# The recurrent block of a five-stage attention network on one Trainium2 core: narrow products in pairs, packed weights, three mixture buffers, another order of units

## The chip, the core and the metric

The kernel runs on one core of one Trainium2 chip. The metric is the device time of one execution in microseconds. Each verdict rests on several runs on the same chip.

## The reference

The network works on x of 8 batches x 256 tokens x 512 features in fp32: cross attention, a channel attention, self attention, cross attention and MLP over tokens, and at last a recurrent block (RWKV-like), which is all that the change touches. Cut to what matters, for one batch (l = 256, e = 512, 32 heads of 16):

```python
xa = ln(x); sx = shift(xa) - xa
xxx = tanh((xa + sx * maa_x) @ maa_w1).reshape(l, 5, 32)       # five ranks of 32
xxx = einsum('lfd,fde->lfe', xxx, maa_w2)                      # the narrow products M
xk, xw, xv, xr, xg = xa + sx * (maa_stack + xxx)               # the mixtures
w = exp(-exp(time_decay + tanh(xw @ td_w1) @ td_w2))           # D1, and D2 (rank 64)
r, k, v, g = xr @ Wr.T, xk @ Wk.T, xv @ Wv.T, silu(xg @ Wg.T)
# over time, per head: out_t = r_t . (u * k_t v_t + s);  s = k_t v_t + w_t * s
og = group_norm(out) * gn_w + gn_b
x1 = x + (og * g) @ Wo.T
xc = ln(x1); sx2 = shift(xc) - xc
xk2, xr2 = xc + sx2 * ffn_maa_k, xc + sx2 * ffn_maa_r
out = x1 + sigmoid(xr2 @ Wfr.T) * (square(relu(xk2 @ Wfk.T)) @ Wfv.T)
```

## The kernel before

`recurrent_block` runs the five engines as five programs of one order. A batch has 16 **steps** j. Step j handles one row of each head's state: TensorE spreads v (`spread`, L2888, into ps_v), VectorE multiplies by k (L3248) and scans over time with the decay (L3251, into sE), GpSimd multiplies by r (L2762, into rs), TensorE sums over the rows (`sum_rows`, L2899, into ps_acc). A small ScalarE copy (L3111, kT from st, the **seed**) sets the start of the next step's scan; it waits for the multiply of the step (kv_made).

Between the parts of a step stand **units** of other batches, which the schedules name (L2401 to L2431). While batch b steps, the A units prepare batch b + 1 (T: transposes of the normalised rows; XX: tanh of the shared rank product; Mw, Mk, Mr, Mg, Mv: the narrow products and mixtures; D1, D2: the decay; K, R, G, V: the projections; C: the bonus), B units the same for b + 2, Z units finish batch b - 1 (E, Q: group norm; O0, O1; LS, LN: statistics and rows of the second layer norm; T; X, XA, XR: its mixtures xk2 and xr2; FK, FR, FV: the feed-forward part). L units are A units that are still left of batch 0. The digit is the half. Each engine takes its piece of a unit in the order of its own schedule, so a waiting piece holds up all that stands behind it on that engine.

`TENSOR_SCHEDULE` has one string per step. In a step TensorE issues the spread of step j + 1, the first unit, the sum of step j - 1, then the other units (with fewer than two units the sum comes first, `run`, L2540).

The A units share two PSUM banks, ps_a0 and ps_a1, in turn: `place` gives a unit its number, `bank_of` the bank by its parity, and a unit waits for `keeps`, that is, until the unit two places before has been emptied, mostly by ScalarE. The Z units share ps_z. The five mixtures lie in turn in two buffers xm0 and xm1 (`mixed_in`); each is made by ScalarE from the bank (L3017), VectorE's product with sx (L3189) and GpSimd's sum (L2712). `statistics` (VectorE, L3156) makes mean, variance + eps and minus the mean; `power` (GpSimd, L2699) makes 1/sqrt and the shift.

A narrow product has 32 rows (M) or 64 (D2) that matter, but its weights are padded with zeros to 128 rows, and it runs over all of xxT or tdT_xx4:

```python
w2, xx = (m2[:, f, :], xxT) if f < 4 else (t2_m2b[:, 1, :], tdT_xx4)
for j in range(2):
    c = 2 * half + j
    mm = pe.matmul(ps_a[:, j, :], w2[:, c * P:(c + 1) * P], xx[:, :], start=True, stop=True)
```

After the last step all engines run FV0 and FV1 of batch 6, and only then `finish`, which takes batch 7 through group norm, O, layer norm and feed-forward.

## Time and profile before

| | |
|---|---|
| median of three runs | 3763.62 us (3759.48 to 3764.11) |
| the profiled execution | 3758.29 us |
| its span | 3756.5 us |
| TensorE busy | 3456.7 us, 92% |
| VectorE busy | 2375.2 us, 63% |
| GpSimd busy | 2010.2 us, 54% |
| ScalarE busy | 1834.3 us, 49% |
| mean granted TensorE clock | 0.968 of 2.4 GHz |

How to read it: the shares are means over five stages with different limits. The recurrent block begins at about 2764 us with the building of rec_ident and ends the program. The span is that of the engines' work; what lies around it is 1.8 us. Matmuls are pipelined and the trace models their ends, so two that follow each other seem to overlap: the distance between starts, as the chain of waits gives it, is what one costs.

### The profile page before, as it was taken

To read this page: it belongs to the slowest core of one execution; us is meant where nothing else is said; L and a number is where in the kernel's file an instruction comes from. 1 tells how busy PE (TensorE), PEld (TensorE's weight loads), DVE (VectorE), ACT (ScalarE), POOL (GpSimd) and SP (SyncE) were. 2 spreads that over 40 slices of the span, in tenths; PEclk is the share of its full clock that TensorE was granted. 3 is DMA by queue.
4 is the path that set the end of the run, shared out by engine and by line. 5 is a ranking of instruction groups with operands and counts; after the bars stand their busy time and mean duration, and the time that the engine had idled before them with its cause. 6 is when DMAs were issued, how large, how long until landed. Compare 5 with 4: busy or idle time off the path is not lost. (4 is left out here: it accounts for less than half of the span.)

```text
span 3756.5 us, 60351 instructions
## 1 busy us (share of the span) xinstructions
PE 3456.7 (92%) x23802; PEld 2695.1 (72%) x23802; DVE 2375.2 (63%) x2953; ACT 1834.3 (49%) x4242; POOL 2010.2 (54%) x1048
## 2 busy tenths in 40 slices
PE   8989999999999999789989997899987888888968
PEld 6878778777877887478877785788865665666634
DVE  2455565566556556667778786654426777788775
ACT  1145664565466456567666775544432333333322
POOL 2235765565566556345556664454434566666652
PEclk9999999999999999999999999999998999999988
DMA  4231211121121111110121111200030000000000
GB/s 145 90 127 46 81 57 58 57 80 58 46 70 68 58 47 68 63 54 29 35 74 52 45 44 48 86 23 23 23 135 6 12 18 18 1 18 18 12 17 12
DMA packets 114305, 189.95 MB, mean 51 GB/s; under 512 B 17904, under 2 KB 36848, under 8 KB 113392
## 3 DMA queue, kind: packets, MB, share of 16 engines
q1 hardware_dynamic: 111856, 182.00, 14.4%
q8 instruction: 185, 3.03, 0.3%
q10 hardware_dynamic: 2176, 4.19, 0.3%
q14 instruction: 88, 0.72, 0.1%
HBM read 161.01 MB, written 25.17 MB: 50 GB/s over the span
## 5 line engine op out<-in xcount | busy, mean ns | idle before, releaser
L1025 POOL TENSOR_TENSOR l_pr<-l_pr,l_inv 128x1024 f32<-128x1024 f32 x256 | 479.7, 1894 | 383.2 <-DVE l_inv L1087 383.2
L895 ACT ACTIVATE l_pr<-l_ps_s,l_top 128x512 f32<-128x512 f32 x512 | 348.6, 690 | 352.5 <-DVE l_top L1083 272.9
L1529 POOL TENSOR_TENSOR tok_pr<-tok_pr,tok_ma 128x1024 f32<-128x1024 f32 x128 | 304.8, 2404 | 281.2 <-DVE tok_pr L1907 281.2
L2762 POOL TENSOR_TENSOR rec_rs<-rec_sE,rec_rT 128x1024 f32<-128x1024 f32 x128 | 326.3, 2552 | 235.2 <-DVE rec_sE L3251 183.8
L1020 POOL TENSOR_TENSOR l_x_lo<-ahead_piece,l_x_hi 128x1024 fp32r<-128x1024 f32 (+1 forms) x97 | 294.0, 3031 | 154.2 <-ACT l_x_hi L879 154.2
L1083 DVE TENSOR_REDUCE l_top<-l_ps_s 128x2 f32<-128x1024 f32 x256 | 303.9, 1217 | 10.5 <-PE l_ps_s L669 10.5
L3251 DVE TENSOR_TENSOR_SCAN rec_sE<-rec_wE,rec_ps_v 128x1024 f32<-128x1024 f32 x128 | 292.7, 2286 | 5.5 <-POOL rec_rs L2762 1.1
L679 PE MATMUL l_ps_t<-l_ident,l_pr 128*128 128x128 f32 x2048 | 275.4, 277 | 10.7 <-POOL l_pr L1025 4.7
L679 PEld LDWEIGHTS l_ps_t<-l_ident,l_pr 128*128 128x128 f32 x2048 | 225.7, 141 | 78.0 <-issue 60.7
L1779 ACT ACTIVATE tok_pr<-tok_pr,tok_shift 128x256 f32<-128x256 f32 x512 | 253.8, 498 | 15.7 <-DVE tok_shift L1915 14.4
L630 PE MATMUL l_ps_b<-l_x_hi,l_w_lo 128*128 128x256 f32 x784 | 226.7, 289 | 0.0
L630 PE MATMUL l_ps_b<-l_x_hi,l_w_hi 128*128 128x256 f32 x784 | 221.2, 282 | 0.0
L630 PE MATMUL l_ps_b<-l_x_lo,l_w_hi 128*128 128x256 f32 x784 | 221.1, 282 | 0.0
L3248 DVE TENSOR_TENSOR rec_ps_v<-rec_ps_v,rec_kT 128x1024 f32<-128x1024 f32 x128 | 156.7, 1224 | 74.5 <-ACT rec_kT L3111 73.4
L1915 DVE TENSOR_REDUCE tok_shift<-tok_pr 128x4 f32<-128x1024 f32 x128 | 155.5, 1216 | 48.1 <-POOL tok_pr L1529 46.2
L1091 DVE COPY l_pT<-l_ps_t 128x512 f32<-128x512 f32 x256 | 174.2, 680 | 2.9 <-PE l_ps_t L679 2.6
L2173 POOL TENSOR_TENSOR ahead_piece<-ahead_piece 128x512 f32<-128x512 f32 x64 | 92.1, 1440 | 151.0 <-DVE ahead_piece L2350 151.0
L900 ACT ACTIVATE l_pT<-l_ps_t 128x512 f32<-128x512 f32 x256 | 152.6, 596 | 22.8 <-PE l_ps_t L679 22.7
L1615 PE MATMUL tok_ps_t<-tok_ident,tok_pr 128*128 128x128 f32 x1024 | 138.7, 279 | 23.2 <-DVE tok_pT L1920 17.3
L1907 DVE TENSOR_TENSOR tok_pr<-tok_ps_s,tok_mk 128x1024 f32<-128x1024 f32 x128 | 155.6, 1216 | 5.1 <-PE tok_ps_s L1604 4.9
L1615 PEld LDWEIGHTS tok_ps_t<-tok_ident,tok_pr 128*128 128x128 f32 x1024 | 113.6, 142 | 53.3 <-issue 35.1
L657 PE MATMUL l_ps_b<-l_wv_lo,l_x_hi 128*128 128x256 f32 x512 | 149.4, 292 | 1.8 <-DVE l_v_later L1097 0.8
(507 smaller groups left out, 9883.8 us busy)
## 6 DMA issues: line engine op xcount, KB each, us to landing
ahead_piece<-x SPq DMA_DIRECT2D x63, 512.0 KB, 3.8
ahead_piece<-in_c SPq DMA_DIRECT2D x63, 512.0 KB, 4.8
ahead_rows<-x SPq DMA_DIRECT2D x22, 512.0 KB, 4.3
ahead_piece<-in_L_w_qk SPq DMA_DIRECT2D x16, 512.0 KB, 6.3
x<-tok_xb SPq DMA_DIRECT2D x16, 512.0 KB, 2.8
l_xt<-in_xT SPq DMA_DIRECT2D x8, 512.0 KB, 6.3
l_ct<-in_cT SPq DMA_DIRECT2D x8, 512.0 KB, 7.2
l_xn<-in_x SPq DMA_DIRECT2D x8, 512.0 KB, 4.9
```

The source lines that it names most:

```text
L630: mm = pe.matmul(bank[:, here], w[:, part, half * SLOTS + s, :], x[b % 2][:, s, here], start=(s == 0 and w is w_lo), stop=(s == SLOTS - 1 ...
L679: mm = pe.transpose(ps_t[h][:, m, :], pr[t][:, h, m * P:(m + 1) * P], ident[:, :])
L895: act.activation(pr[t][:, h, :], ps_s[:, t % 2, h, :], ACT.Exp, bias=top[:, t, h:h + 1], accum_out=mass[:, t, h:h + 1]).then_inc(exped, 1)
L1020: pool.tensor_tensor(x_lo[b % 2][:, which, :], rows, x_hi[b % 2][:, which, :].bitcast(F32), ALU.subtract).then_inc(x_split, 2 if source is ...
L1025: pool.tensor_tensor(pr[t][:, :, :], pr[t][:, :, :], inv[:, t, :].unsqueeze(2).to_broadcast([P, 2, FEAT]), ALU.mult).then_inc(scaled, 1)
L1083: dve.tensor_reduce(top[:, t, :], ps_s[:, t % 2, :, :], AXIS.X, ALU.max, negate=True).then_inc(topped, 1)
L1091: dve.tensor_copy(pT[1][:, :, t * P:(t + 1) * P], ps_t[1][:, :, :]).then_inc(turned_kept[1], 1)
L1529: pool.tensor_tensor(tile, tile, ma[u][:, :, :].rearrange("p t k -> p (t k)").unsqueeze(1).to_broadcast([P, 2, TT * TOK]), ALU.add).then_i ...
L1615: mm = pe.transpose(ps_t[:, i, t, m * P:(m + 1) * P], pr[n % RING][:, i, m, t * P:(t + 1) * P], ident[:, :])
L1779: ins = act.activation(tile, tile, ACT.Exp, bias=shift[n % RING][:, i, m:m + 1], accum_out=mass[n // 2 % 2][:, m, n % 2 * 2 + i:n % 2 * 2 ...
L2762: pool.tensor_tensor(rs[j % 2][:, :, :], sE[j % 2][:, :, :], rT[s][:, :, :], ALU.mult).then_inc(rs_made, 1)
L3251: dve.tensor_tensor_scan(sE[j % 2][:, :, :].rearrange("p c t -> p (c t)"), wE[s][:, :, :].rearrange("p c t -> p (c t)"), ps_v[j % 2][:, :, ...
```

## The change

- **Pairs.** The M and D2 units are no longer A units of TensorE's own. `few_rows` issues two of them together, Mw with Mk, Mr with Mg, Mv with D2, half by half; each product takes only its own 32 (D2: 64) rows of weights and data, and the two of a pair fill ps_a0 and ps_a1 in turns. At its start it waits for both banks. The other engines still have the single units.
- **Packed weights.** The zero rows go: m2 shrinks from [128, 4, 512] to [128, 512], t2_m2b from [128, 2, 512] to [128, 512].
- **Three mixture buffers**: k and v in xm0, w and g in xm1, r in xm2.
- **New order of units** on all engines, with the bank numbers taken from the order itself (`units_in_order`).
- **Merged spreads.** vs is one tile for both halves, and a spread is two products of 512 columns instead of four of 256. The order of features and `head_rows` follow from that.
- **Statistics.** VectorE's `statistics` loses a copy and two small operations; `power` on GpSimd has four instead of two.
- **Finish.** FV0 and FV1 of batch 6 stand inside `finish`; squares, sx2 and the normalised rows of the last batch lie in mixture buffers, the variance product goes to ps_a1, some filler products go.

```diff
-    A_UNITS = ("T0", "T1", "XX0", "XX1", "Mw0", "Mw1", "Mk0", "Mk1", "D1", "K0", "Mr0", "Mr1", "D20", "D21", "K1",
-               "R0", "Mg0", "Mg1", "R1", "Mv0", "Mv1", "G0", "G1", "V0", "V1", "C")
+    A_UNITS = ("T0", "T1", "XX0", "XX1", "D1", "K0", "K1", "R0", "R1", "G0", "G1", "V0", "V1", "C")
+
+    PAIRS = {"Mwk": ("Mw", "Mk"), "Mrg": ("Mr", "Mg"), "Mvd": ("Mv", "D2")}
+    NARROW_UNITS = tuple(n + h for pair in PAIRS.values() for n in pair for h in "01")
...
-    NA, NZ = len(A_UNITS), len(Z_UNITS)
-    PROLOGUE = "LS LN T0 T1 SX XX0 XX1 Mw0 Mw1 Mk0 Mk1 D1 K0 Mv0 Mv1 D20 D21 K1 V0 Mr0 Mr1 V1"
+    NA, NZ = len(A_UNITS + NARROW_UNITS), len(Z_UNITS)
+    PROLOGUE = "LS LN T0 T1 SX XX0 XX1 Mwk0 Mw0 Mk0 Mwk1 Mw1 Mk1 D1 K0 K1 Mvd0 Mv0 D20 Mvd1 Mv1 D21 V0 Mrg0 Mr0 Mg0 Mrg1 Mr1 Mg1 V1"
     FIRST_TENSOR_SCHEDULE = (
-        "L:Mg0 L:Mg1 L:R0 L:R1", "L:G0", "L:G1 L:C", "A:T0 A:T1", "", "A:XX0 A:XX1", "A:Mw0 A:Mw1 A:Mk0 A:Mk1",
-        "A:D1 A:K0", "A:Mr0 A:Mr1 A:D20 A:D21", "A:K1 A:R0", "A:Mg0 A:Mg1 A:R1", "A:Mv0 A:Mv1 A:G0", "A:G1 A:V0",
-        "A:V1 A:C B:T0 B:T1", "B:XX0 B:XX1", "B:Mw0 B:Mw1 B:Mk0 B:Mk1")
+        "L:R0 L:R1", "A:T0 A:T1", "L:C L:G0", "A:XX0 A:XX1", "L:G1", "A:Mwk0 A:Mwk1", "A:D1 A:Mrg0 A:Mrg1", "A:K0",
+        "A:K1 A:R0", "A:R1", "A:Mvd0 A:Mvd1 A:G0", "A:G1 A:V0", "A:V1", "A:C B:T0 B:T1", "B:XX0 B:XX1", "B:Mwk0 B:Mwk1")
     TENSOR_SCHEDULE = (
-        "A:D1 A:K0", "Z:E A:Mr0 A:Mr1 A:D20 A:D21", "Z:Q A:K1", "A:R0", "A:Mg0 A:Mg1 A:R1", "A:Mv0 A:Mv1", "Z:O0 A:G0",
-        "Z:O1 A:G1", "A:V0", "A:V1 Z:T0", "Z:T1 A:C B:T0 B:T1", "Z:FK0", "Z:FK1 B:XX0 B:XX1", "Z:FR0 B:Mw0 B:Mw1 Z:FR1",
-        "B:Mk0 B:Mk1 Z:FV0", "Z:FV1")
+        "A:D1 A:Mrg0 A:Mrg1", "Z:E A:K0", "A:K1 Z:Q", "A:R0", "A:R1", "A:Mvd0 A:Mvd1", "Z:O0 A:G0", "Z:O1 A:V0", "A:V1",
+        "Z:T0 A:C Z:T1", "A:G1 B:T0 B:T1", "Z:FK0", "Z:FK1 B:XX0 B:XX1", "Z:FR0 B:Mwk0 B:Mwk1 Z:FR1", "Z:FV0", "Z:FV1")
...
     VECTOR_SCHEDULE = (
-        "", "Z:E", "A:Mr1 B:LS", "Z:I", "A:Mg1", "Z:N3", "A:Mv1", "A:G0", "Z:LS A:G1", "A:V0", "A:V1 A:C", "Z:X", "B:SX",
+        "", "Z:E A:Mr1", "B:LS", "Z:I", "A:Mg1", "Z:N3", "A:Mv1", "A:G0", "A:V0 Z:LS", "A:V1", "A:C A:G1 Z:X", "", "B:SX",
         "", "B:Mw1", "B:Mk1 Z:FV0 Z:FV1")
...
-        m1, m2 = sb("m1", [P, FT, 2 * P]), sb("m2", [P, 4, FEAT])
-        t1, t2_m2b = sb("t1", [P, FT, P]), sb("t2_m2b", [P, 2, FEAT])
+        m1, m2 = sb("m1", [P, FT, 2 * P]), sb("m2", [P, FEAT])
+        t1, t2_m2b = sb("t1", [P, FT, P]), sb("t2_m2b", [P, FEAT])
...
-        xm = [sb(f"xm{i}", [P, FT, TOK]) for i in range(2)]
+        xm = [sb(f"xm{i}", [P, FT, TOK]) for i in range(3)]
...
+        squares, normal_rows = xm[1], xm[0][:, :, :].rearrange("p (m a) n -> p m (a n)", m=TT)
...
+        def mixed_in(name):
+            return xm[{"k": 0, "v": 0, "w": 1, "g": 1, "r": 2}[name]]
...
-        vs = [[sb(f"vs{u}{i}", [P, FT, TOK], F32R) for i in range(2)] for u in range(2)]
+        vs = [sb(f"vs{u}", [P, 2, FT, TOK], F32R) for u in range(2)]
...
-            for half in range(2):
-                z_unit(LAST - 1, 1 - LAST % 2, f"FV{half}")
...
+            def few_rows(b, *units):
+
+                half, ranks = int(units[0][2]), []
+                for unit in units:
+                    pe.wait_ge(keeps(b, unit), kept_by(b, unit, 1))
...
+                    f = "kwvrg".index(unit[1]) if unit[0] == "M" else 5
+                    first = f * MIX if f < 4 else DECAY if f == 4 else 0
+                    rows = slice(first, first + (MIX if f < 5 else DECAY))
+                    ranks.append((unit, (m2 if f < 4 else t2_m2b)[rows, :], (xxT if f < 4 else tdT_xx4)[rows, :]))
+                for j in range(2):
+                    c = 2 * half + j
+                    for unit, w2, xx in ranks:
+                        mm = pe.matmul(bank_of(b, unit)[:, j, :], w2[:, c * P:(c + 1) * P], xx, start=True, stop=True)
+                        if j == 1:
+                            mm.then_inc(a_filled, 1)
...
-                for c in range(FT):
-                    mm = pe.matmul(ps_v[j % 2][:, c, :], sel[:, c % 2, j % SUB, :], vs[s][c // 2][:, j // SUB, :],
+                for c in range(FT // 2):
+                    mm = pe.matmul(ps_v[j % 2][:, 2 * c:2 * c + 2, :], sel[:, c, j % SUB, :], vs[s][:, :, j // SUB, :],
                                    start=True, stop=True)
...
-                dve.tensor_copy(var_eps[i][:, :], stats[i][:, :, 2]).then_inc(counted[i], 1)
...
-                dve.tensor_scalar(var_eps[i][:, :], moments[i][:, :, 1], 1e-5, None, ALU.add).then_inc(counted[i], 1)
-                dve.tensor_scalar(shift[i][:, :], moments[i][:, :, 0], -1.0, None, ALU.mult).then_inc(counted[i], 1)
...
+                pool.wait_ge(counted[i], of(b, 2, 1))
                 pool.wait_ge(normalised[i], of(b - 1, 1, 0))
+                pool.tensor_tensor(var_eps[i][:, :], moments[i][:, :, 1], eps[:, :], ALU.add).then_inc(powered[i], 1)
+                pool.wait_ge(powered[i], of(b, 4, 0))
                 pool.tensor_tensor(rstd[i][:, :], var_eps[i][:, :], half_power[:, :], ALU.pow).then_inc(powered[i], 1)
-                pool.wait_ge(powered[i], of(b, 2, 0))
-                pool.tensor_tensor(shift[i][:, :], shift[i][:, :], rstd[i][:, :], ALU.mult).then_inc(powered[i], 1)
+                pool.wait_ge(powered[i], of(b, 4, 1))
+                pool.tensor_tensor(shift[i][:, :], moments[i][:, :, 0], rstd[i][:, :], ALU.mult).then_inc(powered[i], 1)
+                pool.wait_ge(powered[i], of(b, 4, 2))
+                pool.tensor_tensor(shift[i][:, :], shift[i][:, :], minus_one[:, :], ALU.mult).then_inc(powered[i], 1)
...
-                keep_busy(pe, ps_v[1][:, 0, 0:P], ident, 14)
+                z_unit(b - 1, 1 - s, "FV0")
...
                     mm.then_inc(last_o, 1)
+                z_unit(b - 1, 1 - s, "FV1")
+                pe.wait_ge(z_kept, of(b - 1, NZ, z_at("FV0")))
```

Where instructions move, on the engines that wait there:

TensorE, steps 13 and 14 of a batch like 1 to 5, before, from FR0 to FV0. rec_m2 with rec_xxT is a narrow product (first Mw0, Mw1, later Mk0, Mk1; each row is two products), the last digit of rec_ps_a the bank.

```order
L2791 MATMUL rec_ps_z<-rec_w_fr,rec_xr2 128x512 x4
L2899 MATMUL rec_ps_acc<-rec_rs0,rec_spr 32x256 x4
L2820 MATMUL rec_ps_a0<-rec_xxT,rec_m2 128x256 x2
L2820 MATMUL rec_ps_a1<-rec_xxT,rec_m2 128x256 x2
L2791 MATMUL rec_ps_z<-rec_w_fr,rec_xr2 128x512 x4
L2888 MATMUL rec_ps_v1<-rec_vs00,rec_sel 128x256 x2
L2888 MATMUL rec_ps_v1<-rec_vs01,rec_sel 128x256 x2
L2820 MATMUL rec_ps_a0<-rec_xxT,rec_m2 128x256 x2
L2899 MATMUL rec_ps_acc<-rec_rs1,rec_spr 32x256 x4
L2820 MATMUL rec_ps_a1<-rec_xxT,rec_m2 128x256 x2
L2791 MATMUL rec_ps_z<-rec_w_fv,rec_kk 128x512 x4
```

And with the change, from the sum behind FR0:

```order
L2931 MATMUL rec_ps_acc<-rec_rs0,rec_spr 32x256 x4
L2836 MATMUL rec_ps_a0<-rec_xxT,rec_m2 128x256
L2836 MATMUL rec_ps_a1<-rec_xxT,rec_m2 128x256
L2836 MATMUL rec_ps_a0<-rec_xxT,rec_m2 128x256
L2836 MATMUL rec_ps_a1<-rec_xxT,rec_m2 128x256
L2836 MATMUL rec_ps_a0<-rec_xxT,rec_m2 128x256
L2836 MATMUL rec_ps_a1<-rec_xxT,rec_m2 128x256
L2836 MATMUL rec_ps_a0<-rec_xxT,rec_m2 128x256
L2836 MATMUL rec_ps_a1<-rec_xxT,rec_m2 128x256
L2815 MATMUL rec_ps_z<-rec_w_fr,rec_xr2 128x512 x4
L2920 MATMUL rec_ps_v1<-rec_vs1,rec_sel 128x512 x2
L2931 MATMUL rec_ps_acc<-rec_rs1,rec_spr 32x256 x4
```

The four units Mw and Mk stand together between the two FR, in turns on both banks, where two of them stood a step later.

TensorE, steps 9 to 11, before: V1 (w_v), the spread and sum pairs, T0 and T1 (rec_sq), C (hs_u), the transposes of batch b + 2, FK0.

```order
L2784 MATMUL rec_ps_a<-rec_xm,rec_w_v 128x256 x8
L2899 MATMUL rec_ps_acc<-rec_rs,rec_spr 32x256 x4
L2776 MATMUL rec_ps_z<-rec_ident,rec_sq 128x128 x4
L2888 MATMUL rec_ps_v<-rec_vs,rec_sel 128x256 x4
L2776 MATMUL rec_ps_z<-rec_ident,rec_sq 128x128 x4
L2899 MATMUL rec_ps_acc<-rec_rs,rec_spr 32x256 x4
L2835 MATMUL rec_ps_a<-rec_sx,rec_hs_u 32x256 x4
L2776 MATMUL rec_ps_a<-rec_ident,ahead_rows 128x128 x8
L2888 MATMUL rec_ps_v<-rec_vs,rec_sel 128x256 x4
L2899 MATMUL rec_ps_acc<-rec_rs,rec_spr 32x256 x4
L2784 MATMUL rec_ps_z<-rec_xk,rec_w_fk 128x256 x8
```

With the change:

```order
L2800 MATMUL rec_ps_z<-rec_ident,rec_sq 128x128 x4
L2931 MATMUL rec_ps_acc<-rec_rs,rec_spr 32x256 x4
L2868 MATMUL rec_ps_a<-rec_sx,rec_hs_u 32x256 x4
L2800 MATMUL rec_ps_z<-rec_ident,rec_sq 128x128 x4
L2920 MATMUL rec_ps_v<-rec_vs,rec_sel 128x512 x2
L2808 MATMUL rec_ps_a<-rec_xm,rec_w_g 128x256 x8
L2931 MATMUL rec_ps_acc<-rec_rs,rec_spr 32x256 x4
L2800 MATMUL rec_ps_a<-rec_ident,ahead_rows 128x128 x8
L2920 MATMUL rec_ps_v<-rec_vs,rec_sel 128x512 x2
L2931 MATMUL rec_ps_acc<-rec_rs,rec_spr 32x256 x4
L2808 MATMUL rec_ps_z<-rec_xk,rec_w_fk 128x256 x8
L2920 MATMUL rec_ps_v<-rec_vs,rec_sel 128x512 x2
```

G1 (w_g) stands in step 10, between T1 and the products ahead of FK0.

VectorE, from the scan of step 9 on, before: V0 and V1 (rec_vs), C (L3200), X (rec_xk), SX (rec_xm from rec_sx and rec_cols); L3248 and L3251 are a step's multiply and scan.

```order
L3251 SCALAR_TENSOR_TENSOR rec_sE<-rec_wE,rec_ps_v 128x1024
L3195 TENSOR_TENSOR rec_vs<-rec_ps_a,rec_vs 64x2x255 x2
L3248 TENSOR_TENSOR rec_ps_v<-rec_ps_v,rec_kT 128x1024
L3251 SCALAR_TENSOR_TENSOR rec_sE<-rec_wE,rec_ps_v 128x1024
L3195 TENSOR_TENSOR rec_vs<-rec_ps_a,rec_vs 64x2x255 x2
L3200 TENSOR_TENSOR rec_bonus<-rec_bonus,rec_ps_a 128x1024
L3248 TENSOR_TENSOR rec_ps_v<-rec_ps_v,rec_kT 128x1024
L3251 SCALAR_TENSOR_TENSOR rec_sE<-rec_wE,rec_ps_v 128x1024
L3231 SCALAR_TENSOR_TENSOR rec_xk<-rec_sq,rec_cols,rec_xcT 128x256 x4
L3248 TENSOR_TENSOR rec_ps_v<-rec_ps_v,rec_kT 128x1024
L3251 SCALAR_TENSOR_TENSOR rec_sE<-rec_wE,rec_ps_v 128x1024
L3182 SCALAR_TENSOR_TENSOR rec_xm<-rec_sx,rec_cols,rec_xaT 128x256 x4
```

With the change, from the multiply of step 9 on:

```order
L3276 TENSOR_TENSOR rec_ps_v<-rec_ps_v,rec_kT 128x1024
L3279 SCALAR_TENSOR_TENSOR rec_sE<-rec_wE,rec_ps_v 128x1024
L3223 TENSOR_TENSOR rec_vs<-rec_ps_a,rec_vs 64x2x255 x2
L3276 TENSOR_TENSOR rec_ps_v<-rec_ps_v,rec_kT 128x1024
L3279 SCALAR_TENSOR_TENSOR rec_sE<-rec_wE,rec_ps_v 128x1024
L3228 TENSOR_TENSOR rec_bonus<-rec_bonus,rec_ps_a 128x1024
L3234 SCALAR_TENSOR_TENSOR rec_g<-rec_g,rec_ps_a 128x512
L3259 SCALAR_TENSOR_TENSOR rec_xk<-rec_sq,rec_cols,rec_xcT 128x256 x4
L3276 TENSOR_TENSOR rec_ps_v<-rec_ps_v,rec_kT 128x1024
L3279 SCALAR_TENSOR_TENSOR rec_sE<-rec_wE,rec_ps_v 128x1024
L3276 TENSOR_TENSOR rec_ps_v<-rec_ps_v,rec_kT 128x1024
L3279 SCALAR_TENSOR_TENSOR rec_sE<-rec_wE,rec_ps_v 128x1024
```

C, G1 (rec_g) and X stand ahead of step 11's multiply and scan, where X stood behind them; V0 has gone a step earlier, and SX now follows the scan of step 12.

## Rows read from the trace of the kernel before

**Rows 1.** Windows of the recurrent block: us; busy us (and instructions) per engine; granted clock; DMA

```profile
2833.73:2957.80 124.07, 92.97 (x482) 69.08 (x483) 74.23 (x62) 33.51 (x81) 66.03 (x32) 0.87 0.05 14
3209.52:3253.97 44.45, 34.34 (x198) 22.94 (x197) 40.33 (x37) 16.10 (x35) 32.03 (x16) 0.95 0.00 1
3253.97:3320.95 66.98, 66.12 (x316) 46.64 (x317) 47.28 (x38) 23.39 (x53) 39.13 (x19) 0.96 0.08 25
3209.52:3320.95 111.43, 100.46 (x514) 69.58 (x513) 87.61 (x74) 39.50 (x88) 71.16 (x35) 0.95 0.05 15
3513.80:3614.44 100.64, 89.98 (x474) 60.67 (x472) 76.74 (x60) 31.83 (x71) 62.99 (x31) 0.97 0.03 11
```

**Rows 2.** The scans by tile: ns min/median/max, first and last start

```profile
L3251 DVE TENSOR_TENSOR_SCAN rec_sE<-rec_wE,rec_ps_v x128: 2285/2286/2289, 2823.5 to 3690.6; 128x1024 f32<-128x1024 f32 x128
```

**Rows 3.** Timeline of TensorE: start, us, operation, [idle before, released by]

```profile
3253.97 6.58 PE L2784 MATMUL rec_ps_z<-rec_xk,rec_w_fk 128*128 128x256 f32 x16 [7.14 <-DVE rec_xk L3231]
3325.76 3.67 PE L2791 MATMUL rec_ps_z<-rec_w_o,rec_bonus 128*128 128x512 f32 x8 [0.47 <-DVE rec_bonus L3223]
```

**Rows 4.** The chain of waits in one batch: start, us, engine, tile, line

```profile
3269.66 3.43 PE rec_ps_z L2791 x8
3273.66 1.93 PE rec_ps_a L2820 x8
3303.80 0.47 PE rec_ps_v L2888 x4
3304.27 1.73 PE rec_ps_z L2861 x8
3306.00 0.57 PE rec_ps_acc L2899 x8
3306.57 3.65 PE rec_ps_a L2784 x16
```

**Rows 5.** Groups by line, TensorE: x count | busy us, mean ns | idle before

```profile
L1604 PE MATMUL tok_ps_s<-tok_kT,tok_qT 32*128 32x256 f32 x1024 | 73.4, 400 | 0.0
L2820 PE MATMUL rec_ps_a<-rec_xxT,rec_m 128*128 128x256 f32 x256 | 66.9, 394 | 3.3 <-DVE rec_vs L3195 2.3 <-ACT rec_tdT_xx L3026 0.6
```

**Rows 6.** Timeline of ScalarE

```profile
3274.76 1.70 ACT L3017 ACTIVATE rec_xm<-rec_ps_a,rec_cols 128x256 f32<-128x256 f32 x4 [1.03 <-PE rec_ps_a L2820]
```

**Rows 7.** Timeline of VectorE

```profile
3231.35 0.99 DVE L3162 COPY rec_var_epsz<-rec_statsz 128x2 f32<-128x2 f32 x1
3248.46 5.37 DVE L3231 SCALAR_TENSOR_TENSOR rec_xk<-rec_sq,rec_cols,rec_xcT 128x256 f32<-128x256 f32 x4
3257.21 1.65 DVE L3182 SCALAR_TENSOR_TENSOR rec_xm<-rec_sx,rec_cols,rec_xaT 128x256 f32<-128x256 f32 x4
```

**Rows 8.** Timeline of GpSimd

```profile
3251.08 2.07 POOL L2717 TENSOR_TENSOR rec_sx<-rec_xaT 128x1024 f32<-128x1024 f32 x1
```

**Rows 9.** Timeline of TensorE in the prologue

```profile
2778.22 5.41 PE L2810 MATMUL rec_ps_a<-rec_xm,rec_m 128*128 128x256 f32 x16 [2.52 <-DMA rec_mean_of<-in_L_group_mean]
```

**Rows 10.** DMA of 2755 to 2850: GB/s in 40 slices; issues, KB, us to landing

```profile
GB/s 0 0 130 91 7 31 213 417 366 379 389 385 387 392 393 383 386 392 382 188 4 0 0 0 0 0 0 0 0 0 7 0 0 0 0 0 0 0 0 0
rec_m<-in_L_maa_w SPq DMA_DIRECT2D x1, 1024.0 KB, 6.4
rec_t_m2b<-in_L_td_w SPq DMA_DIRECT2D x1, 512.0 KB, 7.2
```

**Rows 11.** The chain of waits in the tail

```profile
3698.38 3.70 PE rec_ps_z L2791 x8
3702.07 3.43 PE rec_ps_a L2791 x8
3710.48 1.98 PE rec_ps_z L2934 x8
3716.11 8.84 PE rec_ps_v L2941 x16
```

**Rows 12.** Waits of 2830 to 3700: waiting line <- releaser: us, times, longest

```profile
ACT rec_kT L3111 <- DVE rec_ps_v L3248: 106.3, 29, 9.0
```

162 lines of the change are left out of this document (82 added, 80 removed), and 9 rows, old and new, of tables (FIRST_SCALAR_SCHEDULE, SCALAR_SCHEDULE).

## The prediction

> **What bounds the kernel now.** The diff touches only the last of the five stages, the recurrent block, so I read that stage alone. First the busy time by window [rows 1], then the scans' span [rows 2]: 128 scans (eight batches of sixteen steps) run from 2823.5 to 3690.6 us. What comes before 2823.5 is the stage's prologue, what comes after 3692.8 its tail. Five of the eight batches (1 to 5) are alike; one of them, cut at the same multiply of step 5, is 111.43 us, and the windows divide it into two stretches of unlike kind. In 44.45 us from the multiply of step 5 to the first FK product (call it the **middle**), VectorE is busy 40.33 and TensorE 34.34. In the other 66.98 us (the **dense** stretch) TensorE is busy 66.12 and VectorE 47.28. So each batch pays VectorE and its chains first, then TensorE.
>
> The TensorE timeline shows where the two meet [rows 3]: it sits idle for 7.14 us until VectorE has made xk, and then FK0 takes 6.58 us where an equal unit takes 3.65 [rows 4], because the clock was lower after the idle time. FK0 starts at 3253.97 and the next O0 at 3325.76: 71.8 us. The rest of the batch, O0 to FK0, is 111.4 - 71.8 = 39.6 us.
>
> **Part 1: narrow products in pairs.** A batch has 24 narrow products (M and D2); eight instructions for four of them take 1.93 us [rows 4], so all take 11.6. Do two products over different rows overlap? The token attention has four 32-row products in flight: 1024 instructions, 73.4 us, 72 ns each, against 66.9/256 = 261 ns here [rows 5]. I therefore take a pair half (eight instructions, two products deep) at 1.0 us, bounds 0.6 and 1.93. But both banks ps_a0 and ps_a1 now fill together, and the second half of a pair waits until ScalarE has emptied both. ScalarE takes 1.70 us for two units [rows 6]. A pair is then 1.0 + 1.85 (1.70 and the signals) + 1.0 = 3.85 us: just what its four units take today, where one bank is emptied while the other fills. **So I credit the pairs with nothing**; what hides ScalarE's 1.7 us today is the next narrow unit. Only the sum of a step (0.57 us [rows 4]) stands between the halves of Mvd; between those of Mwk and Mrg stands nothing.
> The Trainium skill, TensorEngine Tiling (Array Packing), section PSUM Bottleneck, says that tiling speeds up TensorE but not the emptying of PSUM; its Theoretical Speedup table would have 4x for 32 rows. By the table alone two in flight would halve the 11.6 us; this case's row for four in flight (261 against 72 ns) bears the speed-up of the products out, and says nothing of the emptying.
>
> **Part 2: the dense stretch.** In the new order from FK0 to O0 stand: FK0, FK1, XX (3.65 each with both XX), FR and FV (four of 3.43), Mwk and Mrg (3.85 each), D1, E, Q (1.73 each), K and R (four of 3.65), Mvd (about 4.2 with its sum), eleven spreads of 0.47 and ten sums of 0.57 [rows 4], and 0.6 us between FK0 and FK1: 67.3 us at full clock. Two waits are new. FV1 stands one step after FV0 and waits until VectorE has emptied ps_z, which stands behind a scan and the product of Mk: 0.8. XX0 waits for the mixing of SX, which stands two scans behind X: 0.6. That makes 68.7 against 71.8 today. Of FK0's 2.9 us of slow clock half stays by my choice (bounds 0 and 2.9), since the new order has shorter idle spells ahead of it: 70.1. Gain 1.7.
>
> **Part 3: the middle.** Today xk is made in step 11, after that step's multiply and scan, and its four operations take 5.37 us with GpSimd's SX subtraction (2.07) running beside them [rows 7, 8]; the four equal ones of SX, alone, take 1.65 [rows 7]. Now X is in step 10, and SX comes a step later on GpSimd, behind a product that needs the next scan: nothing runs beside X. G1 (3.65) moves from step 7 into the gap. LS loses its copy (0.99 [rows 7]) and two tiny operations to GpSimd. Walking it from O0 at 0: O0 3.4, G0 7.6, O1 11.5, V0 15.7 (all TensorE, back to back). VectorE has finished scan 8 at 12.5 and waits for ScalarE's copies of V0 until 17.6; V0, the add and LS follow until 21.1; rstd and shift 22.8; the rows 24.4; TensorE, which had finished V1 at 20.4, waits for T0 about 3 us; T1 until 26.9, xcT 27.9. GpSimd does its product of step 10 first (scan 10 ends at 29.5), so sx2 is ready at 33.8, xk at 35.5, FK0 at 35.6. Against 39.6: gain 4.0. The idle time ahead of FK0 falls from 7.1 to about 2.4 us. A batch is 70.1 + 35.6 = 105.7 us, gain 5.7, five times: **28.5**. Batch 6 (100.64 [rows 1]) has no next-but-one batch: I take 4. Batch 7 keeps its order, LS alone is shorter: 1.
>
> **Part 4: prologue and batch 0.** m2 falls from 1024 to 256 KB, t2 from 512 to 256: 1 MB less in the queue at some 385 GB/s [rows 10] is 2.7 us, of which TensorE waited 2.52 [rows 9]: gain **2.5**. With pairs the first mixture is emptied after both halves' banks and comes 1.9 later; V0 now stands behind Mvd and its mixture (about 4.5), and Mrg stands ahead of V1. The walk puts the first product of GpSimd (2833.73 today) 5.0 later against the weights. Batch 0 from there to batch 1's scan is 124.07 us at a granted clock of 0.87, with TensorE busy 92.97 [rows 1] at that clock; Mg is already done, R stands first, and XX, D1, K lie closer to what they wait for. By the same walk it is 106; the bounds are 124 (nothing) and 95. I take 108: gain 16.1. Net of the 5.0, prologue and batch 0 give **13.6** with the DMA.
>
> **Part 5: the tail.** FV0 and FV1 of batch 6 (3.70 + 3.43, and the 0.69 ahead of them) stand in the chain today [rows 11]. FV0 now goes between the variance product (ends 3712.46) and O (starts 3716.11), a gap of 3.66; FV1 between O and the transposes, a gap of about 3.2 that it overfills by some 0.5. Gain 7.3; bounds 4 and 9 (O at 8.84 instead of 6.86 is clock again). **7.3.** That squares and normal_rows now lie in mixture buffers only lifts waits for sq. The third buffer xm2 and the merged spreads I cost at nothing: two of 512 columns stream as many columns as four of 256, and the 0.47 us [rows 4] hide their weight loads already; if half the instructions cost or save 0.05 us a step, that is 6 us over 128 steps either way, inside the range.
>
> **The sum.** 28.5 + 4 + 1 + 13.6 + 7.3 = 54.4 us against the profiled execution (3758.29, its span 3756.5): 3703.9. The median of the runs is 5.3 above it: 3709. The walk leaves out small signals, which I leave inside the range.
>
> **Rivals.**
> (a) *The middle keeps its length.* VectorE's 40.33 of 44.45 us speaks for it: the chain over V0, LS and T0 is now serial. Then 5 x 4.0 fall out: 3729. Against it speaks the move of X out of GpSimd's way.
> (b) *The evacuation hides.* If ScalarE empties in step with the pair, or the slow clock goes entirely, a batch gains another 1.85 x 2 + 1.4 = 5.1, six times 31: 3678.
> (c) *Pairs don't overlap.* Each half costs up to 0.9 more, 6 x 6 x 0.5 (half of it lies under ScalarE's work): 3727.
> The Trainium skill's same page, section Key Properties, says that changing the tiling mode drains TensorE; Mvd mixes 64 and 32 rows, and by that rule (c) would hold for Mvd at least. No row of before shows a 32-row product beside one of 64. In numbers, Mvd alone without overlap is 6 x 2 x 0.9, 11 us at most: 3720, part of (c).
> (d) *Slower.* ScalarE is in order, and its seed copy waits for VectorE's multiply: 29 waits, 106.3 us, the longest 9.0 [rows 12]. If such a wait stands ahead of the emptying of Mwk and Mrg, both banks stay full and TensorE stops, at two places in each of six batches. From 5.3 us a place the whole gain is gone; at 9.0, 108 us: 3817. Against it: in my walk the seed of step 0 is through just as D1 ends.
> (e) *It does little:* the packing saves bytes only and the waits move: within 7.5 us.
>
> **How the numbers follow.** My forecast 0.57, (a) 0.14, (b) 0.12, (c) 0.08, (d) 0.05, (e) 0.04. A measurement of this kernel tells about 0.2%, 7.5 us, from no change. Faster: 0.57 + 0.14 + 0.12 + 0.08 = 0.91. Same 0.04, slower 0.05. The range takes in (a) to (c) and the bounds of batch 0 (8 us up, 13 down) and the clock: 3675 to 3745.
>
> **What would show it.** Right: a batch of 104 to 107 us between equal multiplies; idle ahead of FK0 of 2 to 3 us; xk's four operations in 1.7 us; about 1.9 us of idle TensorE between halves of Mwk and Mrg, put down to ScalarE; XX0 of batch 0 some 2.5 us earlier; FV0 of batch 6 after the variance product. Wrong: a batch above 110, pair halves at 1.9 us, or long idle times ahead of a pair put down to ScalarE behind its seed copy. The forecast falls as a whole if batch 0 does not shrink by at least 8 us and the middle not by 2.

## The result and the profile after

The changed kernel is **slower**, by 1.6%: 3821.4 us median (3814.3 to 3828.0, 4 runs) against 3761.7 (3759.5 to 3764.1) for the kernel before on the same chip, a ratio of 1.0158, interval [1.0138, 1.0178]. Forecast were 3709 us and a range up to 3745. The profiled execution is 3821.81 us, its span 3820.0, at a granted clock of 0.954 (before: 0.968).

The windows of the recurrent block after the change, cut at the first scan of a batch and at FK0 and O0 (columns as in [rows 1]):

```profile
2843.02:2982.65 139.63, 102.31 (x478) 69.52 (x476) 82.09 (x67) 34.26 (x85) 63.14 (x34) 0.79 0.05 12
3304.00:3386.62 82.62, 71.89 (x319) 44.93 (x319) 60.97 (x43) 26.29 (x61) 51.61 (x26) 0.91 0.07 20
3386.62:3423.47 36.85, 32.63 (x164) 20.51 (x162) 23.17 (x26) 13.13 (x28) 19.29 (x13) 0.93 0.00 1
3304.00:3423.47 119.47, 104.52 (x481) 65.44 (x481) 84.14 (x68) 39.43 (x88) 70.90 (x39) 0.91 0.05 14
```

A middle batch takes 119.5 us instead of 111.4. The middle (third row) is 36.85 us, where 35.6 was forecast and [rows 1] and [rows 3] give 39.6 for before; the dense stretch (second row) is 82.6 us instead of 71.8, and its clock 0.91 instead of 0.96. Both profiles, cut at the first scan of every batch, give the whole account: 19.5 us are lost up to the first scan of batch 0 (3.3 of them before this stage begins, at 2767.5 instead of 2764.2 us), 5.4 in batch 0, 14.0 in batch 1, 4 x 8.6 in batches 2 to 5, 3.2 in batch 6; batch 7 gains 3.7 and the tail 9.2. Sum 63.5, the difference of the spans.

The timeline of TensorE in one dense stretch (start, us, operation, idle before and its releaser):

```profile
3374.87 0.82 PE L2920 MATMUL rec_ps_v<-rec_vs,rec_sel 128*128 128x512 f32 x2
3375.95 0.67 PE L2836 MATMUL rec_ps_a<-rec_xxT,rec_m 32*128 32x256 f32 x2 [0.27 <-issue]
3376.55 0.70 PE L2836 MATMUL rec_ps_a<-rec_tdT_xx,rec_t_m2b 64*128 64x256 f32 x2
...
3381.04 1.19 PE L2836 MATMUL rec_ps_a<-rec_xxT,rec_m 32*128 32x256 f32 x2 [1.53 <-ACT rec_wE L3065]
3382.16 1.22 PE L2836 MATMUL rec_ps_a<-rec_tdT_xx,rec_t_m2b 64*128 64x256 f32 x2
...
3386.62 4.59 PE L2815 MATMUL rec_ps_z<-rec_w_o,rec_bonus 128*128 128x512 f32 x8
...
3436.91 5.13 PE L2857 MATMUL rec_ps_a<-rec_xm,rec_m 128*128 128x256 f32 x16 [4.77 <-DVE rec_xm L3210]
...
3446.43 1.13 PE L2836 MATMUL rec_ps_a<-rec_xxT,rec_m 32*128 32x256 f32 x8
3449.31 1.38 PE L2836 MATMUL rec_ps_a<-rec_xxT,rec_m 32*128 32x256 f32 x8 [1.75 <-ACT rec_xm L3050]
3450.62 5.10 PE L2815 MATMUL rec_ps_z<-rec_w_fr,rec_xr 128*128 128x512 f32 x8
```

Four things are to be seen. Mwk's first half (3446.43) takes 1.13 us for eight instructions, and 1.75 us of idle time follow: the pair runs side by side, and waits, as forecast. Mvd (3375.95) does not: its 32-row and 64-row products take turns, four rows of 0.6 to 0.7 us, 2.47 in all. XX0 waits 4.77 us for VectorE. And behind every such place the work runs wholly or in part at the lower clock level (1.2 of 2.4 GHz): the second half of Mvd 4.6 us, O0 4.59, XX 5.13, FR1 5.10, where [rows 4] has 3.43 and 3.65. The wait of XX0 is explained by VectorE and GpSimd (same columns):

```profile
3421.65 1.67 DVE L3259 SCALAR_TENSOR_TENSOR rec_xk<-rec_sq,rec_cols,rec_xcT 128x256 f32<-128x256 f32 x4 [0.41 <-POOL rec_sq L2758]
3431.12 5.64 DVE L3210 SCALAR_TENSOR_TENSOR rec_xm<-rec_sx,rec_cols,rec_xaT 128x256 f32<-128x256 f32 x4 [0.88 <-POOL rec_sx L2737]
```

```profile
3431.04 2.17 POOL L2761 TENSOR_TENSOR rec_xr<-rec_xr,rec_xcT 128x1024 f32<-128x1024 f32 x1
3433.17 2.52 POOL L2782 TENSOR_TENSOR rec_rs<-rec_sE,rec_rT 128x1024 f32<-128x1024 f32 x1
```

The slow mix has changed places: xk, 5.37 us before [rows 7], takes 1.67 with GpSimd idle, and SX, 1.65 before, now takes 5.64 beside XR and rs. The prologue (timeline of TensorE; rec_t is D1, rec_w_v V0 and then V1, rec_sel the first spread):

```profile
2779.90 3.62 PE L2857 MATMUL rec_ps_a<-rec_xm,rec_m 128*128 128x256 f32 x16
...
2793.78 3.75 PE L2862 MATMUL rec_ps_a<-rec_xm,rec_t 128*128 128x256 f32 x8 [5.44 <-POOL rec_xm L2732]
2817.62 5.86 PE L2808 MATMUL rec_ps_a<-rec_xm,rec_w_v 128*128 128x256 f32 x16 [3.80 <-POOL rec_xm L2732]
2832.57 5.23 PE L2808 MATMUL rec_ps_a<-rec_xm,rec_w_v 128*128 128x256 f32 x16 [0.90 <-ACT rec_xm L3050]
2840.99 1.19 PE L2920 MATMUL rec_ps_v<-rec_vs,rec_sel 128*128 128x512 f32 x4 [3.19 <-DVE rec_vs L3223]
```

XX0 no longer waits for DMA (2.52 us in [rows 9]), so that gain came. It is lost to longer waits behind the pairs (D1 5.44 us, where it waited 2.53 before; V0 3.80, none before) and to V1, which starts 9 us behind V0's end.

### The profile page after: what moved, and what is told of

Same layout as the page of the kernel before. It is cut to its first block and busy times, and to the rows that moved or that the text cites. A ratio compares the mean times of both kernels' runs of the same rounds, so it can differ in the third digit from the quotient of the medians.

```text
span 3820.0 us, 59797 instructions
## 1 busy us (share of the span) xinstructions
PE 3488.4 (91%) x23516; PEld 2661.9 (70%) x23516; DVE 2354.0 (62%) x2908; ACT 1833.3 (48%) x4242; POOL 2012.2 (53%) x1079
```

## The experiments

The theory behind the first runs: the loss is made of (A) Mvd's products of unlike size taking turns, (B) the SX mix beside GpSimd, (C) TensorE's lower clock behind narrow products and waits, (D) the prologue's order. The rival: the narrow products are harmless and the new order as such costs the time. Of every run the table gives the median, the ratio to the kernel before with its interval, the mean length of batches 2 to 5 from first scan to first scan, and the granted clock of the profiled run; "on" is the kernel that was edited.

| run | on | edit | us | ratio [95%] | batch | clock |
|---|---|---|---|---|---|---|
| before | | | 3761.7 | 1 | 110.9 | 0.968 |
| after | | | 3821.4 | 1.0158 [1.0138, 1.0178] | 119.5 | 0.954 |
| e1 | after | Mg over 64 rows | 3853.3 | 1.0248 [1.0228, 1.0269] | 123.8 | 0.952 |
| e2 | after | SX earlier, XR later | 3821.9 | 1.0164 [1.0146, 1.0183] | 119.4 | 0.952 |
| e3 | after | pairs not alternated | 3836.5 | 1.0204 [1.0185, 1.0223] | 122.9 | 0.950 |
| e4 | before | narrow, unpaired | 3776.1 | 1.0046 [1.0028, 1.0064] | 112.8 | 0.962 |
| e5 | after | Mv over 64 rows | 3798.1 | 1.0112 [1.0095, 1.0129] | 116.1 | 0.959 |
| e6 | after | work between halves | 3829.5 | 1.0188 [1.0171, 1.0205] | 121.8 | 0.953 |
| e7 | before | X a step earlier | 3749.2 | 0.9965 [0.9951, 0.9979] | 109.9 | 0.970 |
| e8 | before | new end | 3749.4 | 0.9971 [0.9959, 0.9982] | 111.0 | 0.968 |
| e9 | before | e7 + e8 | 3745.6 | 0.9966 [0.9952, 0.9980] | 109.9 | 0.969 |
| e10 | e9 | SX earlier | 3727.7 | 0.9916 [0.9899, 0.9932] | 107.1 | 0.970 |
| e11 | e5 | SX earlier | 3778.1 | 1.0057 [1.0040, 1.0074] | 112.7 | 0.959 |
| e12 | e11 | prologue, FR1 between | 3757.7 | 0.9994 [0.9984, 1.0003] | 108.5 | 0.964 |
| e13 | e12 | selection copy first | 3759.6 | 0.9989 [0.9978, 1.0000] | 108.6 | 0.961 |
| e14 | e10 | spreads, statistics | 3712.9 | 0.9864 [0.9847, 0.9881] | 104.1 | 0.971 |
| e15 | e10 | statistics alone | 3712.6 | 0.9871 [0.9855, 0.9888] | 104.2 | 0.973 |
| e16 | e14 | narrow, unpaired | 3744.6 | 0.9947 [0.9930, 0.9964] | 109.3 | 0.963 |

**e1: 64 rows for Mg, beside Mr's 32.**

```
-  rows = slice(first, first + (MIX if f < 5 else DECAY))
+  rows = slice(first, first + (MIX if f < 4 else DECAY))
```

> The changed kernel, with one slice made longer: the Mv products contract over rows 64 to 127 (their weights are zero below row 95) instead of rows 64 to 95, so that both members of the pair Mvd have 64 rows. Theory: the pair with 32 rows beside 64 does not run side by side (8 instructions 2.47 us in the profile after, where Mwk and Mrg take 1.1), and the loss there is about 1.3 us for the first half and 1 to 3 us for the second, 4.6 us at half clock, in 7 batches: both halves 1.1 to 1.3 us at full clock, the kernel 10 to 25 us under the changed one, 3797 to 3812 us. Rival (the two halves are limited by their waits for ScalarE, not by the tiles): halves still 1.9 to 2.5 us and the time within 4 us of 3821.

The expectation named the wrong unit: in this table f = 4 is g, so Mg got 64 rows (64 to 127, zero weights below its 32) and Mvd kept its sizes. Mr has rows 96 to 127, so the two now also share rows. Mrg, 32 beside 32 in the changed kernel, takes turns exactly like Mvd:

```profile
3370.43 0.67 PE L2836 MATMUL rec_ps_a<-rec_xxT,rec_m 32*128 32x256 f32 x2
3371.02 0.70 PE L2836 MATMUL rec_ps_a<-rec_tdT_xx,rec_t_m2b 64*128 64x256 f32 x2
3371.65 0.69 PE L2836 MATMUL rec_ps_a<-rec_xxT,rec_m 32*128 32x256 f32 x2
3372.27 0.70 PE L2836 MATMUL rec_ps_a<-rec_tdT_xx,rec_t_m2b 64*128 64x256 f32 x2
```

From 1.1 to 2.5 us a half, and the kernel 32 us slower. Whether the unlike counts or the shared rows make this pair take turns, e1 alone can't tell; Mvd (rows 64 to 95 beside 0 to 63) shares none and takes turns too, and e5 below settles it. Alternating costs more (0.62 us a pair of instructions) than two padded 128-row ones (0.48).

**e2: the SX mix out of GpSimd's way.** GpSimd's SX subtraction to step 10, XR to step 12, VectorE's SX to step 11.

```
   GPSIMD_SCHEDULE
-  "Z:X", "B:SX Z:XR", "",
+  "Z:X B:SX", "", "Z:XR",
   VECTOR_SCHEDULE
-  "A:C A:G1 Z:X", "", "B:SX",
+  "A:C A:G1 Z:X", "B:SX", "",
```

> The changed kernel, with the XX mix moved: GpSimd's subtraction SX from step 11 to step 10 behind X, its addition XR from step 11 to step 12, VectorE's SX from step 12 to step 11. Theory: VectorE's SX took 5.64 us because GpSimd ran XR and rs at the same time, and XX0 waited 4.77 us for it and then ran at half clock: the wait goes, XX0 and XX1 take some 3.6 us instead of 5.1, so 4 to 6 us of each of the five middle batches and 3 of batch 0, and the time is 20 to 30 us under the changed kernel, 3791 to 3801. Rival (TensorE is late anyway, and the wait only moves to FV0 or to the spread of the next step; or the mix is only slow elsewhere): under 8 us gained.

The wait of XX0 went (3430.02 below), and the rival was right: nothing was gained. The timeline of TensorE of this run:

```profile
3348.09 1.22 PE L2920 MATMUL rec_ps_v<-rec_vs,rec_sel 128*128 128x512 f32 x2
3349.12 3.62 PE L2893 MATMUL rec_ps_z<-rec_bonus,rec_mean_of 128*128 128x256 f32 x8
...
3430.02 3.72 PE L2857 MATMUL rec_ps_a<-rec_xm,rec_m 128*128 128x256 f32 x16
...
3436.59 3.67 PE L2815 MATMUL rec_ps_z<-rec_w_fr,rec_xr 128*128 128x512 f32 x8 [2.39 <-POOL rec_xr L2761]
```

FR0 now waits 2.39 us for the late XR, and E behind Mrg takes 3.62 us instead of 1.89: the lower clock has moved to a place that had been spared.

**e3: pairs issued one unit after the other.**

```
-  for j in range(2):
-      for unit, w2, xx in ranks:
+  for unit, w2, xx in ranks:
+      for j in range(2):
```

> The changed kernel with the two members of a pair issued one after the other instead of alternately; everything else stays. If alternation is what lets the narrow products run side by side, a half of Mwk or Mrg takes 1.9 us or so instead of 1.1, and the time grows by 2 times 2 halves times 0.8 us in 7 batches, 0 to 22 us, above 3821 (the copies of the first member start earlier, which takes some back). If the alternation costs (half clock behind a pair, Mvd slow), the second half of Mvd and the first FR1 come back to full clock and the time falls by 5 to 20 us.

Alternation is not what makes products run side by side. Mr and Mg, issued one after the other, still start together:

```profile
3349.92 0.45 PE L2836 MATMUL rec_ps_a<-rec_xxT,rec_m 32*128 32x256 f32 x1
3349.93 0.48 PE L2836 MATMUL rec_ps_a<-rec_tdT_xx,rec_t_m2b 32*128 32x256 f32 x1
```

Mvd's first half falls from 2.47 to about 2.1 us (4 + 4 instructions in turn). Yet the kernel loses 15 us: the second half of Mrg, the spread and E are now at the lower clock (E 3.62) and O0 takes 5.62. The work is no longer; the clock is lower.

**e4: narrow products in the old order.** The kernel before with packed weights and each product over its own rows, nothing paired:

```
-  w2, xx = (m2[:, f, :], xxT) if f < 4 else (t2_m2b[:, 1, :], tdT_xx4)
+  first = f * MIX if f < 4 else DECAY
+  w2, xx = (a[first:first + MIX, :] for a in ((m2, xxT) if f < 4 else (t2_m2b, tdT_xx4)))
```

> The kernel before, with packed weights and each Mw, Mk, Mv, Mr, Mg product over its 32 rows and each D2 product over its 64 rows, one after the other in the old order: the narrow part of the change by itself. Theory (the loss is made by pairs, their waits and the new order): within 8 us of the kernel before, with the weights' shorter load worth 1 to 3 us. Rival (narrow products bring the lower granted clock by themselves): a granted clock below 0.96 over the kernel and 15 to 40 us slower than before, in the stretch with O0, FR and the M units.

17 us slower than before (3758.6 on that chip), at a clock of 0.962. The narrow products take as long as the padded ones at full clock (1.99 us for eight), but behind them the clock falls; D2, and Q after it, which takes 1.89 in the kernel before:

```profile
3312.97 2.43 PE L2830 MATMUL rec_ps_a<-rec_tdT_xx,rec_t_m2b 64*128 64x256 f32 x8 [0.64 <-ACT rec_xm L3018]
3315.33 1.22 PE L2889 MATMUL rec_ps_v<-rec_vs,rec_sel 128*128 128x256 f32 x4
3316.35 2.60 PE L2862 MATMUL rec_ps_z<-rec_sq,rec_mean_of 128*128 128x256 f32 x8
```

This is the rival I had set against the theory, and it holds: narrow products bring the lower clock by themselves. The clock is not the whole loss, though: laid beside the kernel before, a batch of e4 also has some twelve places, next to the narrow products, where about 0.1 us is lost at full clock, 1.2 us in all; waits of 1.2 us ahead of O0 and the transposes go in exchange.

**e5: Mv over 64 rows.** v and g change places in the packed arrays, so that Mv lies behind the decay rows and, with zero weights below its 32, fills 64 rows beside D2's 64.

```
-  f = "kwvrg".index(unit[1]) if unit[0] == "M" else 5
+  f = "kwgrv".index(unit[1]) if unit[0] == "M" else 5
-  rows = slice(first, first + (MIX if f < 5 else DECAY))
+  rows = slice(first, first + (MIX if f < 4 else DECAY))
```

> The changed kernel with the weights of the mixtures v and g exchanged in the packed arrays: Mv now lies behind the decay rows and is contracted over 64 rows (zero weights below the 32nd), beside D2 over the other 64 rows; Mg takes its place among the 32-row products, so Mrg stays 32 beside 32. (The run e1 had lengthened Mg and not Mv: its halves of Mrg went from 1.1 to 2.5 us, and the kernel lost 32 us.) If two 64-row products run side by side, a half of Mvd takes 1.2 us at full clock instead of 2.47: 1.3 us less in each half, perhaps 2.5 with a second half at half clock, 2.5 to 4 us in each of 7 batches: 3793 to 3804 us. If 64-row products take turns, the halves stay at 2.2 to 2.5 us and the time within 5 us of 3821. A third outcome: side by side, but the clock falls earlier (less busy) and eats the gain: within 8 us.

As expected, 23 us less. This is the clean test of the row counts: the two products share no rows here nor in the changed kernel, and only the count of Mv differs. Mvd's half is one group of eight, and O0 behind it is at full clock:

```profile
3361.45 1.14 PE L2836 MATMUL rec_ps_a<-rec_tdT_xx,rec_t_m2b 64*128 64x256 f32 x8 [0.27 <-issue]
3365.72 1.13 PE L2836 MATMUL rec_ps_a<-rec_tdT_xx,rec_t_m2b 64*128 64x256 f32 x8 [2.56 <-ACT rec_wE L3065]
3367.36 3.60 PE L2815 MATMUL rec_ps_z<-rec_w_o,rec_bonus 128*128 128x512 f32 x8
```

**e6: other work between the halves.**

```
-  "A:D1 A:Mrg0 A:Mrg1", "Z:E A:K0", ... "Z:FR0 B:Mwk0 B:Mwk1 Z:FR1"
+  "A:D1 A:Mrg0", "Z:E A:Mrg1 A:K0", ... "Z:FR0 B:Mwk0 Z:FR1 B:Mwk1"
```

> The changed kernel with other work between the two halves of a pair: Mrg0, spread, E, sum, Mrg1 and Mwk0, FR1, Mwk1 in the five middle batches (and in batch 6 and 7 as far as they hold them). Theory (TensorE has nothing to issue while ScalarE copies the first half, 1.7 us twice in a batch, and the clock granted behind these places is half): both waits of 1.7 us go, the slow FR1 (5.1 us) comes back to 3.6, E may wait 0.7 us for VectorE; 3 to 5 us of each middle batch, 3796 to 3806 us. Rival (the narrow products alone bring the half clock): waits go, 3 us a batch, but FR1 or what follows stays slow somewhere: 3806 to 3815. Slower than 3821 if FV0 or T0 wait for ScalarE's later copies.

8 us slower than the changed kernel. At Mwk it works: FR0 to FV0 takes 11.1 us instead of 14.4, 1.1 of it given back before FV1. At Mrg the wait only moves behind the pair, and grows, because K0 needs the banks:

```profile
3359.45 5.41 PE L2808 MATMUL rec_ps_a<-rec_xm,rec_w_k 128*128 128x256 f32 x16 [2.70 <-ACT rec_xm L3050]
```

**e7: only X a step earlier, in the kernel before.**

```
-  "A:V1 A:C", "Z:X", "B:SX",
+  "A:V1 A:C Z:X", "", "B:SX",
```

> The kernel before with VectorE's X mix one step earlier (step 10 instead of 11), the part of the new order that shortened the middle. Theory: xk takes 1.7 us instead of 5.4, the idle time before FK0 falls from 7.1 us to 2 to 4 and FK0 keeps a faster clock: 3 to 5 us of each of 6 middle batches, 3732 to 3745 us against 3760. Rival: the SX mix becomes the contended one (5.6 us instead of 1.65, as in the changed kernel) and XX0 waits; then 3752 to 3770.

12 us faster in the medians, with runs from 3741.8 to 3756.0; in the profiled one, the slowest of them, 7 us are gone between the first scan and the end. Theory and rival show at once: FK0's idle time falls from 7.14 to 1.74 and FK0 is at full clock; and the old kernel now has the changed kernel's wait, to the hundredth:

```profile
3363.56 3.69 PE L2784 MATMUL rec_ps_z<-rec_xk,rec_w_fk 128*128 128x256 f32 x16 [1.74 <-DVE rec_xk L3231]
3377.00 5.15 PE L2810 MATMUL rec_ps_a<-rec_xm,rec_m 128*128 128x256 f32 x16 [4.77 <-DVE rec_xm L3182]
```

**e8: only the new end**, the finish of the changed kernel (FV0 and FV1 of batch 6 in it, squares and rows in mixture buffers) in the kernel before.

> The kernel before with the changed kernel's end alone: FV0 and FV1 of batch 6 moved into the finish where TensorE waits, with their squares and rows in the mixture buffers. Theory: the tail behind the last scan shrinks from 66 us to 57 to 59, as in the changed kernel; the time falls by 7 to 9 us to 3750 to 3753. Rival: nothing or under 3 us, since the changed tail gained from something else (the order ahead of it).

12 us less in the medians. By its trace the tail, from the last scan's start, is 56.4 us instead of 66.0, FV0 and FV1 standing around O, which itself takes 7.13 instead of the 8.84 of [rows 11]:

```profile
3704.99 3.60 PE L2795 MATMUL rec_ps_z<-rec_w_fv,rec_kk 128*128 128x512 f32 x8
3708.81 7.13 PE L2944 MATMUL rec_ps_v<-rec_w_o,rec_bonus 128*128 128x512 f32 x16 [0.23 <-DVE rec_bonus L3290]
3715.78 3.60 PE L2795 MATMUL rec_ps_v<-rec_w_fv,rec_kk 128*128 128x512 f32 x8
```

**e9: e7 and e8 together.**

> The kernel before with both earlier pieces, X one step earlier and the new end (e7 and e8 were 12 us faster each). If the two gains lie in different places they add up: 3733 to 3742 us. If they overlap, 3743 to 3750.

3745.6, in the second case: less than the sum. By its trace both pieces are there (batches as in e7, a tail of 57.8 us), but its first scan is at 2825.9 instead of 2821.7 in e8; the stages ahead vary by some us from run to run, so the total can't tell overlap from sum. The stretch from the first scan to the end can: it is 7.3 us shorter than before in e7, 7.1 in e8 and 15.1 in e9, so there the two add up.

**e10: SX earlier, on e9.**

```
   GPSIMD_SCHEDULE
-  "Z:X", "B:SX Z:XR", "", "Z:FK1"
+  "Z:X B:SX", "Z:XR", "", "Z:FK1"
   VECTOR_SCHEDULE
-  "A:V1 A:C Z:X", "", "B:SX",
+  "A:V1 A:C Z:X", "B:SX", "",
```

> The kernel of e9 with the SX subtraction on GpSimd at step 10 behind X, the addition XR alone at step 11, and VectorE's SX mix at step 11. Theory: in e7, as in the changed kernel, VectorE's SX mix took 5.64 us beside GpSimd's work and XX0 waited 4.77 us for it; started one step earlier it still takes up to 5.6 us but ends before XX0's turn, so the wait and the half clock behind it go: 4 to 6 us of 5 batches below e9, 3708 to 3722 us. Rival (as in e2): the slow mix delays the products of step 12 or X itself meets the subtraction, and FK0 and the scans take the wait over: within 5 us of e9.

18 us below e9. XX0's wait is gone; part of the slowness has moved to xk, which now meets the subtraction (3.31 us; 1.67 in the changed kernel), so FK0 waits longer than in e7 and runs partly at the lower clock:

```profile
3353.21 5.37 PE L2788 MATMUL rec_ps_z<-rec_xk,rec_w_fk 128*128 128x256 f32 x16 [3.36 <-DVE rec_xk L3235]
```

**e11: the same move of SX on e5** (XR stays at step 11, unlike e2).

> The kernel of e5 (Mv over 64 rows beside D2) with the same move of SX, XR left at step 11. Theory: XX0's wait of 4.77 us goes, since XR no longer comes late as it did in e2 (there FR0 waited 2.39 us for it): 4 us in each of 5 middle batches, 3773 to 3783 us. Rival: a slower clock elsewhere takes it back, as in e2: 3790 to 3800.

20 us below e5, as expected.

**e12: V1 ahead of Mrg in the prologue, FR1 between Mwk's halves, on e11.**

```
-  V0 Mrg0 Mr0 Mg0 Mrg1 Mr1 Mg1 V1
+  V0 V1 Mrg0 Mr0 Mg0 Mrg1 Mr1 Mg1
-  "Z:FR0 B:Mwk0 B:Mwk1 Z:FR1"
+  "Z:FR0 B:Mwk0 Z:FR1 B:Mwk1"
```

> The kernel of e11 with V1 ahead of Mrg in the prologue and FR1 between Mwk0 and Mwk1 in the middle batches. Theory: in the prologue V1 was held behind both halves of Mrg and their copies (V0 ended 20 us before the first scan); step 0 of batch 0 starts 6 to 9 us earlier. FR1 between the halves was worth 3.3 us a batch in e6 at that place, with 1.1 us given back before FV1: 2 us in 5 batches. Together 12 to 19 us under e11, 3756 to 3770 us: no better than the kernel before even then, though the three faults are mended. Rival: batch 0 takes the start back (Mg is needed later anyway): 5 to 10 us under e11.

20 us below e11, but from one of the two edits: the batches fell by 4.2 us each, twice what I had expected, and the first scan did not move (2842.5). The timeline of TensorE shows why; GpSimd copies the selection matrix only behind its additions for Mr and Mg:

```profile
2840.00 2.05 PE L2920 MATMUL rec_ps_v<-rec_vs,rec_sel 128*128 128x512 f32 x4 [8.58 <-POOL rec_sel L2773]
```

**e13: that copy ahead of the addition for Mr, on e12.**

> The kernel of e12 with GpSimd's copy of the selection matrix (1.04 us) ahead of its addition for Mr of batch 0 instead of behind those for Mr and Mg. Theory: in e12 V1 was ready in time, but the first spread waited 8.58 us for this copy; now it starts when Mrg1 is done, and step 0 of batch 0 comes 7 to 9 us earlier. R0 waits for GpSimd's addition for Mr all the same, so batch 0 gives 3 to 6 us back: 3 to 6 us under e12, 3751 to 3755. Rival: R0 alone sets the start, nothing gained, within 2 us of e12.

The cause of that wait is confirmed: the spread starts at 2833.9. But the time is that of e12: the first scan comes 3.9 us sooner, batch 0 gives 2.4 of them back and batch 6 is 2.9 longer at a clock of 0.92 instead of 0.95. R0 waits for GpSimd's addition all the same:

```profile
2833.88 2.08 PE L2921 MATMUL rec_ps_v<-rec_vs,rec_sel 128*128 128x512 f32 x4
2839.42 5.75 PE L2809 MATMUL rec_ps_a<-rec_xm,rec_w_r 128*128 128x256 f32 x15 [3.47 <-POOL rec_xm L2736]
```

**e14: two more pieces of the change on e10**: two spreads of 512 columns with their arrays, and the statistics' small operations on GpSimd.

> The kernel of e10 with two more pieces of the change: two spreads of 512 columns instead of four of 256, with their arrays and the order of the features, and the statistics' small operations on GpSimd instead of VectorE. A step's spread takes 0.82 us in both profiles, so nothing is gained on TensorE; VectorE is freed of three small operations, GpSimd gets two more in the chain ahead of the normalisation. Theory (these pieces hold none of the loss): within 5 us of e10. Rival: the longer chain on GpSimd makes T0 wait and costs 1 to 2 us a batch, 3735 to 3745.

15 us faster, where I had expected under 5. **e15: the statistics alone**, on e10:

```
-  dve.tensor_copy(var_eps[i][:, :], stats[i][:, :, 2]).then_inc(counted[i], 1)
-  dve.tensor_scalar(var_eps[i][:, :], moments[i][:, :, 1], 1e-5, None, ALU.add).then_inc(counted[i], 1)
-  dve.tensor_scalar(shift[i][:, :], moments[i][:, :, 0], -1.0, None, ALU.mult).then_inc(counted[i], 1)
```

> The kernel of e10 with the statistics' small operations on GpSimd, spreads unmerged. If the statistics are the cause (VectorE's copy of 0.99 us gone from the chain ahead of T0 and G1, O0's wait of 0.47 and the spread's of 0.26 gone, FK0 behind a shorter wait and so at full clock: 3.69 instead of 5.37 us), all of e14's gain is here: 3709 to 3717 us. If the merged spreads are the cause: 3723 to 3730.

All of the gain is here, and the spreads are worth nothing, as forecast. Laid beside e10, a batch loses 1.65 us of waits: 0.6 ahead of a spread, 0.3 ahead of O0, 0.5 ahead of FK0, 0.2 at the transposes. The rest of the 2.9 us is FK0's clock: in e10 it takes 5.4 or 6.7 us, in e14 and e15 3.69 and 5.38 in turn, from batch to batch, behind the same idle time. From e14, two batches:

```profile
3239.24 5.38 PE L2799 MATMUL rec_ps_z<-rec_xk,rec_w_fk 128*128 128x256 f32 x16 [2.89 <-DVE rec_xk L3241]
3344.00 3.69 PE L2799 MATMUL rec_ps_z<-rec_xk,rec_w_fk 128*128 128x256 f32 x16 [2.88 <-DVE rec_xk L3241]
```

**e16: e4's edit on e14.**

> The kernel of e14 with packed weights and every M and D2 product over its own rows, unpaired, as e4 did with the kernel before. Theory (a stretch with narrow products is granted a lower clock behind it): slower than e14 by 5 to 25 us, with a granted clock of 0.960 to 0.967 instead of 0.971. Rival (e4's loss hung on a small difference of its timing): within 4 us of e14, or faster by the 1 to 3 us of the shorter load.

32 us slower, and 5.1 us a batch at unchanged waits. FK0, behind the same 2.88, takes 5.38 in all of batches 1 to 5 instead of every second one, and D2, the spread and Q in front of K1 are slow. From its timeline, then two windows of e16, D2 to Q and batch 4, and the same two of e14:

```profile
3305.65 3.01 PE L2845 MATMUL rec_ps_a<-rec_tdT_xx,rec_t_m2b 64*128 64x256 f32 x8 [0.64 <-ACT rec_xm L3033]
3309.60 3.62 PE L2876 MATMUL rec_ps_z<-rec_sq,rec_mean_of 128*128 128x256 f32 x8
3367.73 5.38 PE L2799 MATMUL rec_ps_z<-rec_xk,rec_w_fk 128*128 128x256 f32 x16 [2.88 <-DVE rec_xk L3242]
```

```profile
3305.65:3313.15 7.50, 7.50 (x19) 5.07 (x19) 6.45 (x8) 4.78 (x9) 5.75 (x4) 0.55 0.01 2
3295.84:3405.07 109.23, 103.33 (x482) 67.51 (x480) 82.93 (x67) 39.59 (x89) 71.89 (x40) 0.95 0.05 16
```

```profile
3285.83:3289.94 4.11, 4.11 (x18) 3.33 (x18) 4.08 (x6) 3.51 (x9) 2.43 (x1) 1.00 0.02 4
3276.02:3379.53 103.51, 97.17 (x482) 65.03 (x480) 86.55 (x67) 39.44 (x88) 71.83 (x40) 1.00 0.06 17
```

As many instructions, 6.2 us more of busy TensorE in 5.7 us more of time, 0.95 instead of 1.00 (this batch of e14 is one of the faster kind; the others take 104.8 us at 0.98). Of the 5.1 us, 3.4 lie in D2 to Q at the lower clock, 1.2 in the twelve or so places of 0.1 us that e4 has too, the rest mostly in FK0.

## Why the prediction was wrong

**Part 2, the dense stretch, is the step that failed**: 70.1 us forecast, 82.6 measured, 12.5 us in each middle batch. The terms that missed are Mvd (5.4 us too little), XX0's wait (4.2) and the clock at XX and FR1 (1.4 and 1.5); the smaller ones cancel. Its errors, by the runs:
- *Full clock behind narrow work.* I let FK0 alone keep half of a slow spell and priced all else at full clock. In the profile after, FK0 is at full clock, but the second half of Mvd, the spread behind it, O0, XX, Mwk1 and FR1 are slow. e4 and e16 show that narrow products alone, in two orders, cost 17 and 32 us, mostly through the clock. I had costed the packed products as less work; they are as long, and what follows is longer. No rival held this.
- *Mvd 4.2 us.* With its sum it measures 9.65: 2.47, 1.1 for the sum, 1.5 idle, 4.6. Rival (c) named the mechanism for Mvd, 11 us at most; e5 puts it at 23 us, because the clock comes with it (and e1 a second such pair, one that shares rows, at 32). The Trainium skill (TensorEngine Tiling (Array Packing), section Key Properties) says that a change of tiling mode drains TensorE; the runs agree with it (32 beside 64 takes turns, 2.5 us; 32 beside 32 and 64 beside 64 does not, 1.1), and I should have given it more than part of 0.08.
- *XX0 0.6 us late.* It is 4.77 us late. I had seen that xk was slow because GpSimd worked beside it, and moved only that: with X made early, XR comes early too, beside SX. e7, e10 and e11 (−18 and −20 us) show it. The Trainium skill (SBUF — State Buffer, section Who interferes with whom) has VectorE operations with two SBUF inputs and GpSimd operations that read SBUF lock each other out of a shared port; the rows agree (1.67 alone, 5.64 beside two GpSimd operations, while a scan that reads PSUM keeps 2.29).

The sum of Part 2 also has a slip: its terms make 67.8 us at full clock, not 67.3, so by its own terms the gain was 51.8 us instead of 54.4. In rival (d) that gain is gone from 4.5 us a place, not 5.3, and the bound of 124 us for batch 0 lies 16 us up, not 8. None of this changes the direction.

**Part 1** was right in mechanism: halves of 1.1 us, 1.75 idle between them put down to ScalarE, no net gain. e6 adds that idle time there can be filled only by work that needs neither bank.

**Part 3** was right in mechanism and too large: the middle is 36.85 us, a gain of 2.75 where 4.0 was forecast, and 0.9 of the missing 1.25 is O0 at the lower clock behind Mvd. xk takes 1.67; FK0's idle time (0.48) is shorter than the 2.4 forecast. What it undervalued is the statistics: I gave their 1 us as 1 us, and on e10's order they are worth 15 us, 3 a batch, 1.65 of them in waits and the rest in FK0's clock.

**Part 4** failed: 13.6 us gain forecast, 21.5 us lost within the stage up to batch 1's scan (16.2 + 5.4), and 14 more in batch 1. The DMA's 2.5 came. The 5.0 us for the late V0 were far too little: D1 and V0 each wait for GpSimd behind a pair, V1 stands behind Mrg and its waits (3.27, 1.72 and 0.90 us), and the clock in the first batch's window is 0.79 instead of 0.87. e12 and e13 removed two waits there without a gain; what sets the prologue's length, and batch 1's 14 us (of which e5, e11 and e12 took 12), was not taken apart further.

**Part 5** was right: 9.2 us in the profile, 7.3 forecast, and e8 has it by itself.

The changed kernel holds pieces that pay (X earlier, the new end, the statistics) and pieces that cost more (narrow products, the 32-beside-64 pair, the XR beside SX). With its three faults mended (e12) it only equals the kernel before; without its narrow products, pairs and order of TensorE's units, and with SX moved a step earlier, **e15 and e14 run in 3712.6 and 3712.9 us, 1.3% under the kernel before** and faster than both. Not tried alone: the third mixture buffer, which the pairs need, the new order of TensorE's units, and padded products in the changed kernel. So what the new order costs or gives by itself stays open.

## What to carry to other kernels

Narrower contractions saved TensorE no time in themselves here and cost the clock for what followed. Where two products are to run side by side, give both the same number of rows, if need be with zeros, as e5 does, and no rows in common. When an operation is slow because another engine works beside it, look for what the move puts in its place: here one step's shift sent the same 4 us from X to SX, and one more step's shift (e10, e11) was worth 18 to 20 us. And a small wait ahead of a TensorE stretch has two prices, its own length and the clock behind it: in e15 VectorE has 1 us less to do in a batch, and the batch is 3 us shorter.

## What was unexpected in the hardware

Two products over different equal-sized row groups start together even when each unit's four instructions are issued in a block (starts 3349.92 and 3349.93 in e3): one row group does not hold up the other. The same FK0 behind the same idle time of about 2.88 us runs in 3.69 or 5.38 us, in turn from batch to batch, where the batch's products are padded (e14, e15), and in 5.38 in all of batches 1 to 5 where they are narrow (e16); behind 1.74 us it is fast (e7), behind 3.36 slow (e10). So the idle time ahead of a unit does not decide its clock alone. In batches of one kernel that repeat, the granted clock alternates or locks (1.00 and 0.98 in e14, 0.95 in every middle batch of e16), and one FK0 is worth 1.7 us of a batch by it.
